# Channel mamba and merge on 65 stored columns of a row instead of 69, from compact copies written by the pixel mamba

## The chip, the cores and the metric

The kernel runs on one core of a Trainium2 chip. The metric is the device time of one execution in microseconds (us). All times are medians of several runs unless one execution is named.

## The reference, cut to what matters

A four layer network works on x of shape (4, 64, 128, 128): frequency gates with attention, a Fourier block with experts, a Hartley convolution, and a block of two mambas. The third layer ends by multiplying its result with a mask over the columns, and the fourth layer takes that as its input:

```python
freqs = jnp.fft.fftfreq(W)
mask = (jnp.abs(freqs) <= CUTOFF).astype(y.dtype)   # CUTOFF = 0.25, W = 128
return y * mask                                      # layer 2: 65 of 128 columns stay
...
def step(h, inp):
    dA_t, dBx_t, C_t = inp
    h = dA_t * h + dBx_t
    y = jnp.einsum('bds,bs->bd', h, C_t)
    return (h, y)
...
xs = x.transpose(0, 2, 3, 1).reshape(1, -1, C)              # one sequence of 65536 pixels
ys = mamba_fwd(xs, spa_in_w, ...)                            # "pixel" mamba
spa = silu(group_norm(ys, spa_gn_w, spa_gn_b, GROUPS)) + x
xe = x.transpose(0, 2, 3, 1).reshape(B * H * W, TOKEN, gcn)  # 8 tokens of 8 channels per pixel
ye = mamba_fwd(xe, spe_in_w, ...)                            # "channel" mamba
spe = x + silu(group_norm(ye, spe_gn_w, spe_gn_b, GROUPS))
w = jax.nn.softmax(att_w)
return spa * w[0] + spe * w[1] + x
```

Columns 0 to 32 and 96 to 127 are nonzero, 65 in all. In the other 63 both the input and the mamba outputs that are added are constants or zero; the pixel mamba has to carry its state over them.

## The kernel before

The program is a row of stages with a barrier of all engines behind each. A stage has one instruction stream for each engine, ordered by semaphores. DMAs are issued by SP alone. The last three stages are the ones that the change touches.

The stage before them stores x2 in DRAM with `KEPT = 69` columns for each of the 4 x 128 image rows: columns 0 to 36 and 96 to 127. The four zero columns are there for the pixel mamba: seen from column 96 of one row (`SHIFT = 32` values earlier), a "row" is 32 + 33 nonzero columns, three zero ones, and one column whose state update is replaced by a jump over the zero part of the image.

`spatial_mamba` (tiles `spa_`, the pixel mamba) walks the 512 rows in `NC = 74` chunks of `RA = 7` rows, 483 values for each of 64 channels. A chunk passes through four engines in software pipelining: the helper `stream` takes for every engine a list of (lag, part) and runs part `c - lag` in iteration c; the first `HEAD` iterations and the last ones are written out, those between are a hardware loop with four chunks in a pass. SP's parts are `next_load` (waits until `project_z` of chunk c is done, then loads chunk c + 4 in two DMAs into slot s = c % 4 of `xt`) and, three chunks behind, `store` (waits until ACT has copied the output to `res`, then writes it to `ys`). PE's parts include `project_x`, `project_out` and, right behind the latter, `project_z`, which reads `xt`; VectorE (DVE) has 16 scans (L2549), 8 products (`feed`, L2535) and one gate in a chunk.

`spectral_mamba` (tiles `spe_`, the channel mamba) treats every stored pixel by itself, in chunks of `GP = 512` pixels that pay no heed to rows: `LX = 4 * 128 * 69 = 35328` pixels are 69 chunks. `HEAD` is 9, so 14 passes of four chunks are in the hardware loop (`(69 - 9) // 4 - 1`), the rest is written out. SP loads one chunk with one DMA and stores one with another. The scans are at L2876, the products at L2865, and PE sums over states with 128x128 matmuls (L2753).

`merge_branches` (tiles `merge_`) holds `ys` and `ye` of all images in SBUF (`v0`, `v1`: eight DMAs of `K = 128 * 69` values in 64 partitions), takes statistics with 24 instructions of `BN = 368` values for each of four parts (L3011), and then in 8 turns of two strips of 16 rows loads x2 again (`xs`), applies the two SiLUs (ACT, L2974), adds (DVE, L3046 to L3056) and stores 16 full rows of 128 columns. The `L = 37` columns on the left and `LR = 32` on the right come from the sum, the 59 between them from a constant that ACT fills in (L2978).

Of the kernel before, what the change touches and what calls it, by code (L numbers as in the profile page):

```python
# [9 lines left out]
ALU = mybir.AluOpType  # L10
# [3 lines left out]
B, C, H, W = 4, 64, 128, 128  # L14
# [1933 lines left out]
M2 = 20  # L1948
KEPT = 69
PADX = 36  # L1950
# [129 lines left out]


LX = B * H * KEPT
ST = 16
TK, CG, DE = 8, 8, 16
TD = TK * DE
# [7 lines left out]

RA = 7
NA = RA * KEPT
NCA = -(-B * H // RA)
LXP = NCA * NA
JUMP = 36
SHIFT = KEPT - JUMP - 1
# [23 lines left out]


def spatial_mamba(nc, x2, w_in, w_conv, w_z, conv_b, w_xd, w_dt, dt_b, w_brep, w_crep, w_b, a_log, a_log2, skip_d, w_out, one_hot, fold, ident,
                  steady, ys):

# [3 lines left out]
    NC, UA, HEAD, NBL, NP = NCA, 4, 10, 16, 8  # L2133
    with Stage(nc, "spa") as st:
# [26 lines left out]
        xt = st.sb("xt", [128, UA, NA + 4])  # L2161
# [14 lines left out]
        res = st.sb("res", [C, 2, NA])  # L2176
# [2 lines left out]
        p_d = [st.ps(f"p_d{i}", [128, 512]) for i in range(4)]  # L2179
        p_u = st.ps("p_u", [128, 2, 512])  # L2180
        x_in, stored = [st.sem(f"x_in{s}") for s in range(UA)], st.sem2("stored")
        (loaded, step, setup_act, setup_pe, w_ready, zeroed, jump_ready, jump_out, jump_in) = (
            st.sem(n) for n in ("loaded", "step", "setup_act", "setup_pe", "w_ready", "zeroed", "jump_ready", "jump_out", "jump_in"))
        (dt_done, x_done, z_done, b_done, c_done, x_read, z_read, soft_step, soft_ready, b_copied, c_copied) = (
# [10 lines left out]
        def rows(t):  # L2195

            return t.rearrange("p (r w) -> p r w", w=KEPT)

        def jumps(t):

# [2 lines left out]
        @block.sync  # L2203
        def _(sp):
            def load(c, s):
                for q in range(2):

                    sp.dma_start(xt[q * C:(q + 1) * C, s, 0:NA + 3], x2[:, bass.ds(c * NA + (PADX - SHIFT - 3 - q), NA + 3)]).then_inc(x_in[s], 16)

            def next_load(c, s, r):  # L2210

                if isinstance(c, int) and c + UA >= NC:
                    return
                sp.wait_ge(z_done, c + 1)
                load(c + UA, s)

            def store(c, s, r):
                sp.wait_ge(out_copied, c + 1)
                sp.dma_start(ys[:, bass.ds(c * NA, NA)], res[:, s % 2, :]).then_inc(stored[s % 2], 16)

            for dst, src in ((wi[:, :, :], w_in), (wc[:, :, :], w_conv), (wz[:, :], w_z), (cb[:, 0:1], conv_b), (wxd[:, :], w_xd),
                             (wdt[:, :], w_dt), (db[:, 0:1], dt_b), (wbr[:, :], w_brep), (wcr[:, :], w_crep), (wb[:, :], w_b), (av[:, :], a_log),
                             (av2[:, :], a_log2), (dd[:, :], skip_d), (wo[:, :], w_out), (hot[:, :, :], one_hot), (fd[:, :, :], fold),
                             (idt[:, :], ident)):
                sp.dma_start(dst, src).then_inc(loaded, 16)
            for s in range(UA):
                load(s, s)

            sp.wait_ge(jump_ready, 1)
            sp.dma_start(steady.rearrange("(d s) -> d s", s=ST), jump[:, :]).then_inc(jump_out, 16)  # L2230
            sp.wait_ge(jump_out, 16)
            with nc.allow_non_contiguous_dma(reason="one column of states at the jump for each pair of strip and rows"):
                for q in range(4):
                    sp.dma_start(jump2[:, 4 * q:4 * q + 4], steady.rearrange("(g q n) -> n q g", g=4, q=4)[:, q, :]).then_inc(jump_in, 16)
            stream(sp, NC, UA, HEAD, 4, (0, next_load), (3, store))
            for s in range(2):
                sp.wait_ge(stored[s], 16 * (NC // 2))

        @block.gpsimd
        def _(pool):  # L2240
# [41 lines left out]
        def _(pe):  # L2282
# [13 lines left out]
                nc.tensor.matmul(p_x[:, 0:NA], wi[:, 1, :], xt[:, s, 1:1 + NA], start=False, stop=True).then_inc(x_done, 1)  # L2296

            def project_z(c, s, r):

                pe.wait_ge(x_read, 2 * c + 2)  # L2300
                nc.tensor.matmul(p_x[:, 0:NA], wz[:, :], xt[0:C, s, 3:3 + NA], start=True, stop=True).then_inc(z_done, 1)

# [263 lines left out]

GP, SUB = 512, 128
NSUB = GP // SUB


def spectral_mamba(nc, x2, w_in, w_conv, w_xd, w_dt, w_bc, dt_b, skip_d, a_wide, a_mask, w_out, ident, ye):
# [1 line left out]

    NC, UE, HEAD = LX // GP, 4, 9
    HALF = DE // 2 * ST * TK
    with Stage(nc, "spe") as st:
        wi = st.sb("wi", [65, 2 * TD])
# [12 lines left out]
        xt = st.sb("xt", [65, UE, GP])  # L2592
# [11 lines left out]
        res = st.sb("res", [C, 2, GP])  # L2604
# [14 lines left out]
        @block.sync  # L2619
        def _(sp):  # L2620
            def load(c, s):
                sp.dma_start(xt[0:64, s, :], x2[:, bass.ds(c * GP + PADX, GP)]).then_inc(x_in[s], 16)

            def next_load(c, s, r):

                if isinstance(c, int) and c + UE >= NC:
                    return
                sp.wait_ge(z_done, c + 1)
                load(c + UE, s)

            def store(c, s, r):
                sp.wait_ge(out_copied, c + 1)
                sp.dma_start(ye[:, bass.ds(c * GP, GP)], res[:, s % 2, :]).then_inc(stored[s % 2], 16)

            for dst, src in ((wi[:, :], w_in), (wc[:, :], w_conv), (wxd[:, :], w_xd), (wdt[:, :], w_dt), (wbc[:, :], w_bc),
                             (db[:, :], dt_b), (dd[:, :], skip_d), (wa[:, :], a_wide), (am[:, :], a_mask), (wo[:, :], w_out), (idt[:, :], ident)):
                sp.dma_start(dst, src).then_inc(loaded, 16)
            for s in range(UE):
                load(s, s)
            stream(sp, NC, UE, HEAD, 4, (0, next_load), (3, store))  # L2640
            for s in range(2):
                sp.wait_ge(stored[s], 16 * ((NC + 1 - s) // 2))
# [247 lines left out]


NR = 16
BN = 368


def merge_branches(nc, ys, ye, x2, gmat, gwb, att, out):

    K = H * KEPT  # L2900
    NS = H // NR // 2
    N = NR * KEPT
    L, LR = JUMP + 1, KEPT - JUMP - 1
    with Stage(nc, "merge") as st:
        v = [st.sb(f"v{q}", [128, 2, K]) for q in range(2)]
        xs = st.sb("xs", [128, 2, N])
# [27 lines left out]
        @block.sync  # L2934
        def _(sp):
            for dst, src in ((gm[:, :], gmat), (gw[:, :, :], gwb), (at[:, 0:2], att)):
                sp.dma_start(dst, src).then_inc(loaded, 16)
            for q, src in enumerate((ys, ye)):
                for a in range(2):
                    for p in range(2):  # L2940
                        sp.dma_start(v[q][64 * p:64 * p + 64, a, :], src[:, (2 * a + p) * K:(2 * a + p + 1) * K]).then_inc(v_in[2 * q + a], 16)  # L2941
            for a in range(2):
                @turns(sp, NS)
                def _(j):
                    for s in range(2):

                        sp.wait_ge(x_scaled[s], a * NS + j)
                        for p in range(2):
                            sp.dma_start(xs[64 * p:64 * p + 64, s, :], x2[:, bass.ds((2 * j + s) * N + (PADX + (2 * a + p) * K), N)])\  # L2949
                                .then_inc(x_in[s], 16)  # L2950
                    for s in range(2):
                        sp.wait_ge(merged[s], a * NS + j + 1)
                        sp.wait_ge(filled[s], a * NS + j + 1)
                        sp.dma_start(ov[:, a, bass.ds((2 * j + s) * NR, NR), :], os[:, s]).then_inc(stored[s], 16)  # L2954
            for s in range(2):
                sp.wait_ge(stored[s], 32 * NS)
# [31 lines left out]
        def _(dve):  # L2988
# [29 lines left out]
            r = K / HW  # L3018
# [20 lines left out]
            for a in range(2):  # L3039
                @turns(dve, NS)  # L3040
                def _(j):
                    for s in range(2):
# [7 lines left out]
                        dve.wait_ge(added[s], a * NS + j + 1)  # L3050

                        dve.wait_ge(stored[s], 16 * (a * NS) + 16 * j)
                        tv = tx[:, :].rearrange("p (r w) -> p r w", w=KEPT)
                        sv = t2[:, s, :].rearrange("p (r w) -> p r w", w=KEPT)
                        nc.vector.scalar_tensor_tensor(os[:, s, :, 0:L], sv[:, :, 0:L], at[:, 4:5], tv[:, :, 0:L], ALU.mult, ALU.add)  # L3055
                        nc.vector.scalar_tensor_tensor(os[:, s, :, W - LR:W], sv[:, :, L:KEPT], at[:, 4:5], tv[:, :, L:KEPT], ALU.mult,  # L3056
                                                       ALU.add).then_inc(merged[s], 1)


# [150 lines left out]
def shape_constants():  # L3210
# [65 lines left out]
    "kd": (B, 99, 1280, BF16), "vd": (B, 128, VC), "den": (4, NH, 512), "qp": (3, B, C, HW, BF16), "x1": (B, C, H, W), "st1": (B, C, 32, 6),  # L3276
    "low1": (2 * MD, B * C, MD), "modes1": (2, B, C, MD, MD), "ab1": (C, 2, B), "y1": (B * C, H, W), "feats": (128, 2, HW),
    "fmean": (128, 2), "sel": (B, TOP, NE), "wts": (B, TOP), "out1": (B, C, H, W), "low2": (2 * MD, B * C, MD),
    "modes2": (2, B, C, M2 + 1, M2 + 1), "x2": (C, NCA * NA + 8), "ys": (C, LXP), "steady": (128 * ST,), "ye": (C, LX),
}  # L3280


# [9 lines left out]
def build(nc, t, out):  # L3292
# [7 lines left out]
    def of(names):  # L3300
        return [t[n] for n in names.split()]
# [19 lines left out]
    hartley_modes(nc, *of("low2 t_re t_im half wm mixc modes2 x2"))  # L3321
    low_inverse(nc, "inv2", t["modes2"], M2 + 1, *of("c_k2 c_m2"), t["x2"][:, PADX:PADX + LX].rearrange("c (b h w) -> h b c w", b=B, h=H))

    spatial_mamba(nc, *of("x2 a_in a_conv a_z a_cb a_xd a_dt a_dtb a_brep a_crep a_b a_alog a_alog2 a_d a_out one_hot fold_states ident steady ys"))
    spectral_mamba(nc, *of("x2 e_in e_conv e_xd e_dt e_bc e_dtb e_d e_alog decay_mask e_out ident ye"))
    merge_branches(nc, t["ys"][:, SHIFT:SHIFT + LX], *of("ye x2 groups16 m_gn m_att"), out)


# [13 lines left out]
```

## Time and profile before

| what | value |
|---|---|
| median of 3 runs | 7990.96 us (7986.05 to 7993.15) |
| the profiled execution | 7999.3 us |
| its span, first to last instruction | 7997.2 us |
| TensorE | 6916.9 us busy, 86% of the span |
| VectorE | 5842.8 us busy, 73% |
| ScalarE | 4018.5 us busy, 50% |
| GpSimd | 3606.3 us busy, 45% |
| pixel mamba, from the first load to the next stage | 3696 to 5753 us, 2057 us |
| channel mamba | 5753 to 7766 us, 2013 us |
| merge | 7766 to 7997.2 us, 231.2 us |

The busy shares are means over all stages. The three stages at the end fill just over half of the span, and each has another limit, so they are read one at a time.

### The profile page before, as it was taken

How to read it: one execution, taken by the hardware profiler on the slowest of the kernel's cores; microseconds unless marked ns; L12 is line 12 of the kernel's file. 1: busy time of each engine (PE TensorE's matmuls, PEld its weight loads, DVE VectorE, ACT ScalarE, POOL GpSimd, SP SyncE). 2: the span in 40 equal slices, each digit the busy share in tenths (PEclk: the TensorE clock that was granted, in tenths of full speed). 3: DMA queues.
4: the chain of work that ended last, by engine and by line, in shares of the span. 5: the costliest groups of instructions: out<-in, count | busy, mean ns of one | idle time of the engine just before them, and what ended most of it. 6: DMA issues, size and time to landing. Idle time of an engine off the chain costs nothing. (4 is left out here: it accounts for less than half of the span.)

```text
span 7997.2 us, 123173 instructions
## 1 busy us (share of the span) xinstructions
PE 6916.9 (86%) x38274; PEld 3725.9 (47%) x38274; DVE 5842.8 (73%) x5708; ACT 4018.5 (50%) x6797; POOL 3606.3 (45%) x2432
## 2 busy tenths in 40 slices
PE   8959479999987369787999999999899999999970
PEld 7845223333335224574222222222277777777760
DVE  4630468777742258213999999999899999999975
ACT  4410456666641357202666666666555555555532
POOL 0100012222210300002777777777688888888860
PEclk9979789999988689756999999999899999999985
DMA  2252443333335623532000000000000000000016
GB/s 71 68 124 46 164 131 100 99 102 100 100 108 123 244 99 103 133 84 46 14 15 13 14 14 13 15 13 14 13 10 11 10 10 10 10 10 11 10 37 188
DMA packets 555088, 500.09 MB, mean 63 GB/s; under 512 B 222861, under 2 KB 462388, under 8 KB 547788
## 3 DMA queue, kind: packets, MB, share of 16 engines
q1 hardware_dynamic: 554763, 495.54, 23.0%
q8 instruction: 232, 3.80, 0.2%
q14 instruction: 93, 0.75, 0.0%
HBM read 328.99 MB, written 163.76 MB: 62 GB/s over the span
## 5 line engine op out<-in xcount | busy, mean ns | idle before, releaser
L2549 DVE TENSOR_TENSOR_SCAN spa_hs<-spa_p_d,spa_hs,spa_bx 128x483 f32<-128x483 f32 x1168 | 1634.5, 1676 | 0.0
L2679 POOL TENSOR_TENSOR spe_hc<-spe_hs,spe_cu 128x1024 f32<-128x1024 f32 x552 | 1291.9, 2361 | 312.5 <-DVE spe_hs L2876 312.5
L2275 POOL TENSOR_TENSOR spa_hc<-spa_hs,spa_cr 128x966 f32<-128x966 f32 x592 | 1223.9, 2068 | 427.7 <-DVE spa_hs L2549 411.6
L2876 DVE TENSOR_TENSOR_SCAN spe_hs<-spe_p_d,spe_bx 128x1024 f32<-128x1024 f32 x552 | 1232.8, 2275 | 46.6 <-ACT spe_p_d L2825 45.9
L2753 PE MATMUL spe_p_y<-spe_idt,spe_hc 128*128 128x128 f32 x8832 | 1036.1, 276 | 0.0
L2753 PEld LDWEIGHTS spe_p_y<-spe_idt,spe_hc 128*128 128x128 f32 x8832 | 1013.9, 193 | 0.0
L1070 DVE TENSOR_REDUCE attention_nm<-attention_p_s 128x2 f32<-128x640 f32 x1024 | 789.2, 812 | 259.2 <-PE attention_p_s L927 258.1
L2535 DVE TENSOR_TENSOR spa_bx<-spa_br,spa_p_u 128x952 f32<-128x952 f32 x592 | 938.2, 1585 | 33.7 <-PE spa_p_u L2345 33.7
L1028 ACT ACTIVATE attention_pr<-attention_p_t 128x512 f32<-128x512 f32 x1280 | 710.6, 598 | 411.7 <-PE attention_p_t L950 285.8
L2825 ACT ACTIVATE spe_p_d<-spe_p_d 128x896 f32<-128x896 f32 x552 | 474.1, 900 | 869.8 <-PE spe_p_d L2738 869.4
L2460 ACT ACTIVATE spa_p_d<-spa_p_d,spa_av 128x483 f32<-128x483 f32 x1184 | 705.1, 634 | 409.8 <-PE spa_p_d L2332 407.7
L2332 PE MATMUL spa_p_d<-spa_du,spa_hot 32*128 32x483 f32 x2368 | 644.4, 619 | 58.0 <-DVE spa_hs L2549 48.8
L2865 DVE TENSOR_TENSOR spe_bx<-spe_cu,spe_p_bc 128x2048 f32<-128x2048 f32 x276 | 631.5, 2288 | 53.4 <-ACT spe_cu L2817 17.0
L2345 PE MATMUL spa_p_u<-spa_du,spa_hot 32*128 32x483 f32 x2368 | 646.9, 621 | 0.6 <-DVE spa_bx L2535 0.5
L927 PE MATMUL attention_p_s<-attention_ks,attention_qs 96*128 96x320 bf16 x2048 | 454.5, 303 | 37.2 <-DMA attention_qs<-scratch_qp 21.1
L1133 POOL TENSOR_TENSOR attention_on<-attention_os,attention_rc 128x512 f32<-128x512 f32 x128 | 162.3, 1268 | 602.4 <-DMA attention_rc<-scratch_den 381.6
L2332 PEld LDWEIGHTS spa_p_d<-spa_du,spa_hot 32*128 32x128 f32 x2368 | 182.0, 184 | 523.1 <-DVE spa_hs L2549 360.6
L967 PE MATMUL attention_p_o<-attention_pr,attention_vs 128*32 128x512 f32 x3072 | 410.0, 606 | 0.4 <-ACT attention_os L1042 0.4
L2738 PE MATMUL spe_p_d<-spe_wa,spe_dt 32*128 32x512 f32 x2208 | 386.8, 640 | 16.9 <-issue 14.0
L950 PE MATMUL attention_p_t<-attention_qs,attention_ks 99*128 99x512 bf16 x1024 | 395.7, 387 | 4.8 <-DMA attention_qs<-attention_mr 3.3
L1902 PE MATMUL experts_p_x<-experts_fs,experts_wx 128*128 128x512 f32 x768 | 331.8, 595 | 47.6 <-DVE experts_bx L1928 47.6
L2359 PE MATMUL spa_p_y<-spa_hc,spa_fd 128*32 128x483 f32 x2368 | 303.6, 585 | 5.4 <-POOL spa_hc L2275 4.2
(423 smaller groups left out, 10807.0 us busy)
## 6 DMA issues: line engine op xcount, KB each, us to landing
attention_qs<-scratch_qp SPq DMA_DIRECT2D x768, 64.0 KB, 2.6
attention_rc<-scratch_den SPq DMA_DIRECT2D x128, 256.0 KB
scratch_qp<-queries_parts SPq DMA_DIRECT2D x96, 256.0 KB, 2.5
spa_xt<-scratch_x SPq DMA_DIRECT2D x148, 121.5 KB, 2.6
front_xs<-in_x_dram SPq DMA_DIRECT2D x64, 256.0 KB, 2.9
scratch_xf<-front_out SPq DMA_DIRECT2D x64, 256.0 KB, 2.3
queries_xs<-scratch_xf SPq DMA_DIRECT2D x32, 512.0 KB, 4.5
attention_xs<-in_x_dram SPq DMA_DIRECT2D x128, 128.0 KB, 4.2
```

The source lines that it names most:

```text
L1028: nc.scalar.activation(pr[:, v, :], p_t[v % 2][:, :], ACT.Exp, scale=HD ** -0.5).then_inc(exp_done[v % 2], 1)
L1070: nc.vector.tensor_reduce(nm[:, c.u, t, 2 * s:2 * s + 2], p_s[s][:, :, 0:NK], AX.X, ALU.max, negate=True).then_inc(s_max[s], 1)
L2275: nc.gpsimd.tensor_tensor(hc[:, k % 8:k % 8 + 2, :], hs[:, k:k + 2, :], cr2[:, s % 2, :].unsqueeze(1).broadcast_to([128, 2, NA]), ALU.mult ...
L2332: mm = nc.tensor.matmul(p_d[(2 * j + e) % 4][:, 0:NA], hot[v, j // 2, :], du[v, s % 2, 0, :], start=True, stop=True)
L2345: mm = nc.tensor.matmul(p_u[:, e, 0:NA], hot[v, j // 2, :], du[v, s % 2, 1, :], start=True, stop=True)
L2460: nc.scalar.activation(p_d[k % 4][:, 0:NA], p_d[k % 4][:, 0:NA], ACT.Exp, scale=av2[:, k:k + 1]).then_inc(decay_ready, 1)
L2535: nc.vector.tensor_tensor(kept(bx[:, 2 * j:2 * j + 2, :]), b, kept(p_u[:, :, 0:NA]), ALU.mult).then_inc(bx_ready, 1)
L2549: nc.vector.tensor_tensor_scan(hs[:, k, v], p_d[k % 4][:, v], bx[:, k, v], 0.0 if start else hs[:, k, NA - 1:NA], ALU.mult, ALU.add).then_ ...
L2679: nc.gpsimd.tensor_tensor(hc[:, k, :, d, :].rearrange("p s d t -> p d s t"), hs[:, k % 2, d, :, :], rows, ALU.mult)\
L2753: mm = nc.tensor.matmul(p_y[:, px], hc[:, k, n].rearrange("p d t -> p (d t)"), idt[:, :], start=False, stop=(n == ST - 1))
L2865: nc.vector.tensor_tensor(bx[:, k % 2], steps, rows, ALU.mult).then_inc(bx_ready, 1)
L2876: nc.vector.tensor_tensor_scan(hs[:, k % 2, d].rearrange("p d s t -> p (d s t)"), p_d[h][:, :], bx[:, k % 2, d].rearrange("p d s t -> p (d ...
```

## The change

The pixel mamba writes its output `ys` without the four zero columns of each row (`full`, 65 of 69 values; 7 pieces of 65 values for each channel, packed in DRAM), and writes a packed copy of its input, `xf2`, from the slot `xt` in which the chunk stands (`keep_x`). `project_z` waits until that copy has landed, since its completion is what lets `next_load` overwrite the slot. The channel mamba reads `xf2` instead of x2 and has `LF = 4 * 128 * 65 = 33280` pixels, 65 chunks. The merge reads packed `ys`, `ye` and `xf2`; its strips are 16 x 65 values, the statistics run in 20 instructions of 416 values instead of 24 of 368, and the parts of the output row are 33, 63 and 32 columns wide instead of 37, 59 and 32.

```diff
+FULL = KEPT - 4
+NF = RA * FULL
...
         x_in, stored = [st.sem(f"x_in{s}") for s in range(UA)], st.sem2("stored")
+        x_kept = [st.sem(f"x_kept{s}") for s in range(UA)]
...
+        def full(t):
+            return rows(t)[:, :, 0:FULL]
...
             def store(c, s, r):
                 sp.wait_ge(out_copied, c + 1)
-                sp.dma_start(ys[:, bass.ds(c * NA, NA)], res[:, s % 2, :]).then_inc(stored[s % 2], 16)
+                sp.dma_start(ys[:, bass.ds(c * NF, NF)], full(res[:, s % 2, :])).then_inc(stored[s % 2], 16)
+
+            def keep_x(c, s, r):
+                sp.wait_ge(x_in[s], 32 * r + 32)
+                sp.dma_start(xf2[:, bass.ds(c * NF, NF)], full(xt[0:C, s, 3:3 + NA])).then_inc(x_kept[s], 16)
...
-            stream(sp, NC, UA, HEAD, 4, (0, next_load), (3, store))
+            stream(sp, NC, UA, HEAD, 4, (0, keep_x), (0, next_load), (3, store))
             for s in range(2):
                 sp.wait_ge(stored[s], 16 * (NC // 2))
+            for s in range(UA):
+                sp.wait_ge(x_kept[s], 16 * ((NC + UA - 1 - s) // UA))
...
             def project_z(c, s, r):
-
+                pe.wait_ge(x_kept[s], 16 * r + 16)
                 pe.wait_ge(x_read, 2 * c + 2)
...
+LF = B * H * FULL
...
-    NC, UE, HEAD = LX // GP, 4, 9
+    NC, UE, HEAD = LF // GP, 4, 9
...
-                sp.dma_start(xt[0:64, s, :], x2[:, bass.ds(c * GP + PADX, GP)]).then_inc(x_in[s], 16)
+                sp.dma_start(xt[0:64, s, :], x2[:, bass.ds(c * GP, GP)]).then_inc(x_in[s], 16)
...
-BN = 368
+BN = 416
...
-    K = H * KEPT
+    K = H * FULL
     NS = H // NR // 2
-    N = NR * KEPT
-    L, LR = JUMP + 1, KEPT - JUMP - 1
+    N = NR * FULL
+    L, LR = FULL - SHIFT, SHIFT
...
+    nonzero = t["xf2"][:, SHIFT:SHIFT + LF]
+    spectral_mamba(nc, nonzero, *of("e_in e_conv e_xd e_dt e_bc e_dtb e_d e_alog decay_mask e_out ident ye"))
+    merge_branches(nc, t["ys"][:, SHIFT:SHIFT + LF], t["ye"], nonzero, *of("groups16 m_gn m_att"), out)
```

On SP, at the top of the pixel mamba's loop, one chunk, in the kernel before. An ISA row is a wait or a register step, REGISTER_ALU computes an address.

```order
L2116 ISA
L2208 ISA
L2208 DMA spa_xt<-scratch_x 64x486
L2208 REGISTER_ALU
L2208 DMA spa_xt<-scratch_x 64x486
L2218 REGISTER_ALU
L2219 ISA
L2219 DMA scratch_ys<-spa_res 64x483
```

The same place in the changed kernel, up to the copy of the next chunk; `scratch_xf` stands for `xf2` here:

```order
L2118 ISA
L2229 ISA
L2229 DMA scratch_xf<-spa_xt 64x7x65
L2220 REGISTER_ALU
L2214 ISA
L2214 DMA spa_xt<-scratch_x 64x486
L2214 REGISTER_ALU
L2214 DMA spa_xt<-scratch_x 64x486
L2224 REGISTER_ALU
L2225 ISA
L2225 DMA scratch_ys<-spa_res 64x7x65
L2229 ISA
```

The copy stands ahead of the chunk's `next_load`, so behind the store of the iteration before; nothing else on SP moved.

On PE, in the same loop, around `project_z` (it reads `spa_wz`), before:

```order
L2345 MATMUL spa_p_u<-spa_du,spa_hot 128x483 x2
L2365 MATMUL spa_p_y<-spa_y,spa_wo 64x483
L2300 ISA
L2301 MATMUL spa_p_x<-spa_xt,spa_wz 128x483
L2091 REGISTER_ALU
L2332 MATMUL spa_p_d<-spa_du,spa_hot 128x483 x2
```

and in the changed kernel:

```order
L2357 MATMUL spa_p_u<-spa_du,spa_hot 128x483 x2
L2377 MATMUL spa_p_y<-spa_y,spa_wo 64x483
L2311 ISA
L2312 ISA
L2313 MATMUL spa_p_x<-spa_xt,spa_wz 128x483
L2092 REGISTER_ALU
L2344 MATMUL spa_p_d<-spa_du,spa_hot 128x483 x2
```

One row is new, the wait for the copy. The rows of VectorE, ScalarE and GpSimd are as many as before (2046, 2011 and 869): the channel mamba's code is the same, with one pass less of its loop.

## Rows read from the trace of the kernel before

**Rows 1.** The page's first line

```profile
span 7997.2 us, 123173 instructions
```

**Rows 2.** Windows: stretch and its length, busy us of each engine, clock, DMA share, GB/s

```profile
3760.00:5700.00 1940.00, 1882.64 (x8085) 565.60 (x8081) 1939.72 (x1808) 1265.47 (x2094) 1523.41 (x870) 1.00 0.05 13
5850.00:7650.00 1800.00, 1770.66 (x12134) 1343.32 (x12132) 1727.69 (x821) 967.41 (x1579) 1493.46 (x759) 0.99 0.04 10
7768.00:7855.00 87.00, 0.00 (x0) 0.00 (x0) 37.14 (x79) 1.58 (x2) 0.00 (x0) 0.50 1.00 210
```

**Rows 3.** Groups of instructions, channel mamba: busy, mean ns, idle before, releaser

```profile
L2876 DVE TENSOR_TENSOR_SCAN spe_hs<-spe_p_d,spe_bx 128x1024 f32<-128x1024 f32 x552 | 1232.8, 2275 | 46.6 <-ACT spe_p_d L2825 45.9
```

**Rows 4.** Timeline of SP, channel mamba: start, length, DMA issued

```profile
6111.31 0.49 SPq L2622 DMA_DIRECT2D spe_xt<-scratch_x  x1
...
6139.11 0.50 SPq L2622 DMA_DIRECT2D spe_xt<-scratch_x  x1
...
6226.47 0.49 SPq L2622 DMA_DIRECT2D spe_xt<-scratch_x  x1
...
7486.15 0.49 SPq L2622 DMA_DIRECT2D spe_xt<-scratch_x  x1
```

**Rows 5.** Timeline of SP and PE, pixel mamba, one chunk

```profile
4275.73 0.52 SPq L2219 DMA_DIRECT2D scratch_ys<-spa_res  x1
...
4300.01 1.07 PE L2301 MATMUL spa_p_x<-spa_xt,spa_wz 64*128 64x483 f32 x2
...
4302.66 0.52 SPq L2219 DMA_DIRECT2D scratch_ys<-spa_res  x1
```

**Rows 6.** The tile spa_res: its DMA issues and time to landing, min/median/max

```profile
L2219 SPq DMA_DIRECT2D scratch_ys<-spa_res x74: 466/519/603, 3792.2 to 5747.3; - x74
DMA to landing us min/median/max: 2.2/2.3/3.0
```

**Rows 7.** DMA, 3560 to 3680 us, the stage before: packets, MB, share of 16 engines

```profile
q1 hardware_dynamic: 38572, 8.67, 53.5%
```

**Rows 8.** Timeline of SP and PE, start of the pixel mamba

```profile
3717.18 2.02 SPq L2234 DMA_DIRECT2D spa_jump<-scratch_steady  x4
...
3726.40 1.07 PE L2301 MATMUL spa_p_x<-spa_xt,spa_wz 64*128 64x483 f32 x2 [1.39 <-ACT spa_sg L2414]
...
3727.50 1.11 SPq L2208 DMA_DIRECT2D spa_xt<-scratch_x  x2
...
3741.36 1.17 PE L2301 MATMUL spa_p_x<-spa_xt,spa_wz 64*128 64x483 f32 x1 [1.31 <-ACT spa_sg L2414]
```

**Rows 9.** Waits in the pixel mamba, 3760 to 5700 us: us in total, times, longest

```profile
PEld spa_p_d L2332 <- DVE spa_hs L2549: 360.6, 420, 1.1
```

**Rows 10.** The tile spa_xt: SP's register steps at its loads, ns min/median/max

```profile
L2208 SPq MOVE spa_xt<-scratch_x x120: 29/29/29, 3979.0 to 5563.8; - x120
```

**Rows 11.** Timeline, end of the pixel mamba to the next stage's first DMA

```profile
5747.31 0.47 SPq L2219 DMA_DIRECT2D scratch_ys<-spa_res  x1
5753.45 0.35 SPq L2637 DMA_DIRECT2D spe_wi<-in_e_in_dram  x1
```

**Rows 12.** Timeline of DVE, merge, the last statistics

```profile
7855.94 12.26 DVE L3011 BATCH_NORM_STATS2 merge_bs<-merge_v 128x6 f32<-128x368 f32 x24 [9.54 <-DMA merge_v<-scratch_ye]
7868.23 2.79 DVE L3015 BATCH_NORM_AGGREGATE merge_mv<-merge_bs 128x2 f32<-128x144 f32 x4
```

**Rows 13.** Timeline of DVE, merge, one of the 8 turns and the start of the next

```profile
7892.66 0.80 DVE L3046 TENSOR_SCALAR merge_tx<-merge_xs,merge_at 128x1104 f32<-128x1104 f32 x1 [7.22 <-DMA merge_xs<-scratch_x]
7893.49 1.37 DVE L3049 SCALAR_TENSOR_TENSOR merge_tx<-merge_t,merge_at,merge_tx 128x1104 f32<-128x1104 f32 x1
7894.99 0.84 DVE L3055 SCALAR_TENSOR_TENSOR merge_os<-merge_t,merge_at,merge_tx 128x592 f32<-128x592 f32 x1
7895.74 0.74 DVE L3056 SCALAR_TENSOR_TENSOR merge_os<-merge_t,merge_at,merge_tx 128x512 f32<-128x512 f32 x1
...
7907.41 0.80 DVE L3046 TENSOR_SCALAR merge_tx<-merge_xs,merge_at 128x1104 f32<-128x1104 f32 x1 [7.01 <-DMA merge_xs<-scratch_x]
```

More of the change, by code:

```diff
@@ L2125, in spatial_mamba @@
 def spatial_mamba(nc, x2, w_in, w_conv, w_z, conv_b, w_xd, w_dt, dt_b, w_brep, w_crep, w_b, a_log, a_log2, skip_d, w_out, one_hot, fold, ident,
-                  steady, ys):
+                  steady, ys, xf2):
     NC, UA, HEAD, NBL, NP = NCA, 4, 10, 16, 8
@@ L2948, in _ @@
                         for p in range(2):
-                            sp.dma_start(xs[64 * p:64 * p + 64, s, :], x2[:, bass.ds((2 * j + s) * N + (PADX + (2 * a + p) * K), N)])\
+                            sp.dma_start(xs[64 * p:64 * p + 64, s, :], x2[:, bass.ds((2 * j + s) * N + (2 * a + p) * K, N)])\
                                 .then_inc(x_in[s], 16)
@@ L3052, in _ @@
                         dve.wait_ge(stored[s], 16 * (a * NS) + 16 * j)
-                        tv = tx[:, :].rearrange("p (r w) -> p r w", w=KEPT)
-                        sv = t2[:, s, :].rearrange("p (r w) -> p r w", w=KEPT)
+                        tv = tx[:, :].rearrange("p (r w) -> p r w", w=FULL)
+                        sv = t2[:, s, :].rearrange("p (r w) -> p r w", w=FULL)
                         nc.vector.scalar_tensor_tensor(os[:, s, :, 0:L], sv[:, :, 0:L], at[:, 4:5], tv[:, :, 0:L], ALU.mult, ALU.add)
-                        nc.vector.scalar_tensor_tensor(os[:, s, :, W - LR:W], sv[:, :, L:KEPT], at[:, 4:5], tv[:, :, L:KEPT], ALU.mult,
+                        nc.vector.scalar_tensor_tensor(os[:, s, :, W - LR:W], sv[:, :, L:FULL], at[:, 4:5], tv[:, :, L:FULL], ALU.mult,
                                                        ALU.add).then_inc(merged[s], 1)
@@ L3278 @@
     "fmean": (128, 2), "sel": (B, TOP, NE), "wts": (B, TOP), "out1": (B, C, H, W), "low2": (2 * MD, B * C, MD),
-    "modes2": (2, B, C, M2 + 1, M2 + 1), "x2": (C, NCA * NA + 8), "ys": (C, LXP), "steady": (128 * ST,), "ye": (C, LX),
+    "modes2": (2, B, C, M2 + 1, M2 + 1), "x2": (C, NCA * NA + 8), "ys": (C, NCA * NF), "xf2": (C, NCA * NF), "steady": (128 * ST,), "ye": (C, LF),
 }
@@ L3322, in build @@
     low_inverse(nc, "inv2", t["modes2"], M2 + 1, *of("c_k2 c_m2"), t["x2"][:, PADX:PADX + LX].rearrange("c (b h w) -> h b c w", b=B, h=H))
-    spatial_mamba(nc, *of("x2 a_in a_conv a_z a_cb a_xd a_dt a_dtb a_brep a_crep a_b a_alog a_alog2 a_d a_out one_hot fold_states ident steady ys"))
-    spectral_mamba(nc, *of("x2 e_in e_conv e_xd e_dt e_bc e_dtb e_d e_alog decay_mask e_out ident ye"))
-    merge_branches(nc, t["ys"][:, SHIFT:SHIFT + LX], *of("ye x2 groups16 m_gn m_att"), out)
+    spatial_mamba(nc, *of("x2 a_in a_conv a_z a_cb a_xd a_dt a_dtb a_brep a_crep a_b a_alog a_alog2 a_d a_out one_hot fold_states ident steady ys xf2"))
+    nonzero = t["xf2"][:, SHIFT:SHIFT + LF]
+    spectral_mamba(nc, nonzero, *of("e_in e_conv e_xd e_dt e_bc e_dtb e_d e_alog decay_mask e_out ident ye"))
+    merge_branches(nc, t["ys"][:, SHIFT:SHIFT + LF], t["ye"], nonzero, *of("groups16 m_gn m_att"), out)
 def kernel(**inputs):
```

## The prediction

> **What bounds the kernel now.** The last three stages are read apart, from windows inside each. In the pixel mamba VectorE is busy for 1939.72 of 1940 us, first row of [rows 2]: it never waits, so whatever else is added there is free as long as VectorE still never waits. In the channel mamba TensorE is busy for 1770.66 of 1800 us and VectorE for 1727.69, second row: the two are nearly balanced, VectorE's scans lose only 46.6 us to waits in the whole stage [rows 3], and no queue of transfers matters at 10 GB/s. A stage like that is as long as its number of chunks times one period. The merge first waits for memory: DMA share 1.00 at 210 GB/s, third row of [rows 2]. Then VectorE takes statistics of the last part to arrive [rows 12], and after a few short operations come 8 turns that alternate between the load of x and VectorE [rows 13].
>
> **The channel mamba, the main term.** It has 65 chunks instead of 69. Head and tail are written out and stay, so exactly one pass of four chunks leaves the loop. The timeline of its loads gives the price [rows 4]: the first load of a pass is issued at 6111.31 and that of the next at 6226.47; twelve passes lie between 6111.31 and 7486.15, so (7486.15 - 6111.31) / 12 = 114.6 us a pass. Inside a pass one chunk takes 6139.11 - 6111.31 = 27.8 us; four would be 111.2, and the other 3.4 us are the jump back at the end of a pass, which leaves with it. I take -114.6. The bounds are 111.2 (the jump's cost stays somewhere) and 115.2 (6226.47 - 6111.31, a long pass). Nothing in the instructions of a chunk changes, since a chunk is 512 pixels in either kernel.
>
> **The merge.** Its eight big loads carry 8 x 64 x 8832 x 4 B = 18.09 MB before and 8 x 64 x 8320 x 4 B = 17.04 MB after. At 210 GB/s, [rows 2], the 1.05 MB are 5.0 us. The last statistics are 24 instructions in 12.26 us [rows 12], 511 ns each for 368 values. 20 of 416 values take 12.26 x 20/24 = 10.2 us if an instruction costs the same whatever its width, and 12.26 x 8320/8832 = 11.5 if only the values count; I take 11.1 between them, -1.1 (bounds -2.0 and -0.7). The aggregation reads 120 numbers instead of 144: at most 2.79 / 6, I take -0.4. A turn of the loop takes 7907.41 - 7892.66 = 14.75 us [rows 13], of which 7 are VectorE's wait for x. For each strip, L3046 and L3049 run over 1040 instead of 1104 values and L3055 over 528 instead of 592. The slope comes from L3055 and L3056: 0.84 us for 592 and 0.74 for 512 is about 1.2 ns a value. So L3049 and L3055 lose 64 x 1.2 ns = 0.08 us each, L3046 by its proportion 0.80 x 64/1104 = 0.05: 0.21 us a strip, 0.42 a turn. x itself: the two loads of a strip carry 0.565 MB, and 64/1104 of that, 33 KB, goes; only the first strip's loads are waited for, and 33 KB at 210 GB/s are 0.15 us. 0.55 us a turn with rounding down, -4.4 in 8 turns; the bounds are -2.5 (only the bytes count: 66 KB a turn, 0.3 us x 8) and -6.8 (everything shrinks by 64/1104: 14.75 x 0.058 x 8). ACT's fill of 63 columns instead of 59 is not on this chain: ACT has the 7 us for it in which VectorE waits.
>
> **The pixel mamba, what is added.** 74 copies `keep_x`, 74 stores that now have 448 pieces of 260 B instead of 64 of 1932 B, and a wait on TensorE. First the copy. It is issued right behind the store of the iteration before, which is at 4275.73 + 0.52 = 4276.3; `project_z`, which waits for it, starts at 4300.01 [rows 5]. The cover is 23.7 us. SP's wait for `x_in` in front of it costs nothing, for that load was issued three chunks earlier. What does the copy take? A store to DRAM lands in 2.3 us [rows 6]. Small pieces are priced by the stage before, where 38572 packets of 225 B on average took 53.5% of 16 engines for 120 us [rows 7]: 0.535 x 120 x 16 / 38572 = 26.6 ns a packet, so 448 of them on 16 engines are 0.75 us. 2.3 + 0.75 = 3 us against 23.7: hidden, with more than 20 us to spare. Without that cover every us would cost 74. Behind the copy on SP stand the two loads of `next_load`, some 0.6 us later than now, for data needed four chunks later, and the store, whose buffer is wanted two chunks later. In the fill of the pipeline the iterations are shorter: the copy of chunk 0 follows the jump transfers at 3717.18 + 2.02 and has 7 us until 3726.40, and that of chunk 1 follows the loads at 3727.50 + 1.11 and has 12 us until 3741.36 [rows 8]. Both hold 3 us easily.
>
> The wait itself is one more row on TensorE in the loop. The nearest price is a register step of 29 ns [rows 10]. TensorE's weight loads waited 360.6 us for VectorE's scans in the window [rows 9], some 5 us a chunk, so I take 0; two such steps on the path in each chunk would be 4.3 us, my upper bound.
>
> A rule of the Trainium skill speaks against the short pieces. [Rows 7] show 26.6 ns for a packet of 225 B, that is 8.5 GB/s for an engine where the long rows of the merge have 210/16 = 13 GB/s. DMA: Bandwidth & Descriptors, Specifications, says that 512 B or more are needed for line rate and that below this the engine reads, modifies and writes. The trace agrees that short pieces are slower, by a third here. By the row the sum is as it stands; if the rule doubled the price of a packet, the last store would land 0.75 us later still and nothing else would change.
>
> At the end of the stage the last store lands 0.75 us later, and SP waits for it. Between its issue and the next stage there are 6.1 us now [rows 11], of which 2.3 are the landing; the other 3.8 hold the clearing of 41 semaphores by GpSimd and the barrier, so four more semaphores are 0.3 us. Together +1.0 (bounds 0.3 and 1.8).
>
> **The sum.** -114.6 - 5.0 - 1.1 - 0.4 - 4.4 + 1.0 = -124.5 us against the profiled execution of 7999.3 us (span 7997.2 [rows 1]): 7874.8. The median of the runs is 8.3 us below the profiled one, so 7990.96 - 124.5 = 7866.5 us.
>
> **Rivals.**
> The copy is late (slower). If the copy landed after `project_z` is due, TensorE would stand still there with the spreads of the same chunk queued behind it, VectorE would starve, and each us late would cost 74. It decides at a landing 23.7 + 124.5 / 74 = 25.4 us after the issue; at 27 us (3.3 us late) the time is 7866.5 + 244 = 8111. Against it: the packets would have to cost 30 times what [rows 7] show. 3%.
> VectorE is disturbed. Its scans fill the pixel mamba completely, and there are now 148 transfers of short pieces that read SBUF beside them. If that, or the extra row on TensorE, made a chunk 0.2 us longer, it would be 15 us: 7881. For it: nothing in the stage has slack on VectorE. Against it: the stage's DMA share is 0.05 [rows 2], and 2 x 0.75 us in each 26.9 us (4302.66 - 4275.73, [rows 5]) adds as much again. 7%.
> The merge loads run slower. Their rows in DRAM have other lengths (33280 B, and a pitch of 134680 B for `ys` and `xf2` instead of near 143000). At 160 GB/s instead of 210 the 17.04 MB take 106.5 us instead of 86.1 before: 20.4 + 5.0 us are lost from the sum, 7892. For it there is nothing in the rows but that the layout changes. 4%.
> The change doesn't do what it says. Then the loop would run as many passes as before; the chunk count is computed from `LF`, and the order of instructions shows unchanged code for the compute engines, so this needs an error that I don't see. Under 1%, counted with the first.
>
> **How the numbers follow.** The forecast has 86%. Its own bounds: the gains are at most 115.2 + 5.2 + 2.0 + 0.5 + 6.8 - 0.3 = 129.4 (7861.6) and at least 111.2 + 4.6 + 0.7 + 0 + 2.5 - 1.8 - 4.3 = 112.9 (7878.1), where 4.6 and 5.2 are the 1.05 MB at 10% more or less bandwidth on either side. The runs of before scatter by 7 us, half of it to either side; that and the disturbed VectorE widen it to 7857 to 7884. 0.2%, 16 us, is about what a measurement of this kernel can tell from no change. Forecast, disturbed VectorE and slow merge loads all lie far beyond it on the fast side, 97%, of which I keep 1% for a mix that ends near no change. Faster 96%, the same 1%, slower 3%.
>
> **What would show it.** The channel mamba's stage, 2013 us now, should be near 1898 with 27.8 us between loads inside a pass and thirteen passes. The pixel mamba should have VectorE busy for all of a window in its middle, 26.9 us a chunk, and no wait of TensorE for a DMA to `scratch_xf`; the copy's landing should be near 3 us. The merge should be near 220 us with a turn of 14.2. It would be wrong if the pixel mamba's chunks grew, if a pass of the channel mamba had another length under the same code, or if the big loads fell below 210 GB/s.

## The result, and the profile after

The changed kernel takes 7900.06 us (median of 4 runs, 7894.98 to 7901.65), the kernel before 7988.51 (4 runs); the ratio is 0.9888 with a 95% interval of 0.987 to 0.9905. It is faster by 88.5 us, where 124.5 were forecast, and the time lies above the range of 7857 to 7884. The profiled execution of after has a span of 7893.2 us.

From the first DMA of one stage to the first of the next (`spa_wi`, `spe_wi`, `merge_gm`), and the forecast for each:

| stage | before | after | change | forecast |
|---|---|---|---|---|
| all before the pixel mamba | 3695.2 | 3677.8 | -17.4 | 0 |
| pixel mamba | 2058.2 | 2061.6 | +3.4 | +1.0 |
| channel mamba | 2012.0 | 1932.9 | -79.1 | -114.6 |
| merge | 231.8 | 220.9 | -10.9 | -10.9 |

The first line is code that both kernels share, and the two profiled executions stand on different sides of their medians (7999.3 against 7988.51, 7894.98 against 7900.06). The other three add up to -86.6, and that is the 88.5 of the medians within 2 us. So the merge came out as worked out, the pixel mamba nearly so, and the channel mamba gave 35.5 us less than one pass of its loop.

The channel mamba's loads in the timeline of SP, as in [rows 4]:

```profile
6100.77 0.48 SPq L2635 DMA_DIRECT2D spe_xt<-scratch_xf  x1
...
6128.60 0.49 SPq L2635 DMA_DIRECT2D spe_xt<-scratch_xf  x1
...
6217.68 0.49 SPq L2635 DMA_DIRECT2D spe_xt<-scratch_xf  x1
```

A chunk inside a pass still takes 6128.60 - 6100.77 = 27.8 us, but a pass takes 6217.68 - 6100.77 = 116.9, and over ten passes from 6067.52 to 7243.34 the mean is 117.6 (before, between the same loads, 114.55). Four chunks in a row are 111.5, so the jump back costs 6.1 us a pass instead of 3.0 (the prediction has 3.4, since it counts four times 27.8 us, where four chunks take 111.5). Twelve intervals that are 3.1 us longer are 37 us: the part that is missing.

The timeline of TensorE shows where. First the kernel before, at the top of a pass:

```profile
6208.47 1.13 PE L2738 MATMUL spe_p_d<-spe_wa,spe_dt 32*128 32x512 f32 x4 [1.19 <-issue]
6209.53 0.90 PE L2726 MATMUL spe_p_bc<-spe_wbc,spe_xz 128*128 128x256 f32 x2
```

and the changed one:

```profile
6197.94 1.13 PE L2751 MATMUL spe_p_d<-spe_wa,spe_dt 32*128 32x512 f32 x4 [1.17 <-issue]
6200.90 1.19 PE L2739 MATMUL spe_p_bc<-spe_wbc,spe_xz 128*128 128x256 f32 x2 [1.84 <-issue]
```

"issue" is idle time in which the engine waited for no semaphore that the profile shows. Before there is one such gap behind the jump, after there are two. VectorE, which is busy for nearly all of a pass, then stands still until ScalarE has the next decay. The waits of VectorE's scans, in us, times and the longest, first before (6000 to 7600 us), then after (6000 to 7500 us):

```profile
DVE spe_hs L2876 <- ACT spe_p_d L2825: 38.1, 14, 3.5
DVE spe_hs L2889 <- ACT spe_p_d L2838: 62.0, 14, 5.8
```

In both executions there are transfers of the kind "instruction" in every pass. The DMA view of the changed kernel, 6067 to 6525 us (four passes of 117.6 less a little), has the same row as that of the kernel before, 6080 to 6538 us:

```profile
q8 instruction: 36, 0.59, 0.5%
```

36 packets of 0.59 MB / 36 = 16.4 KB, nine in a pass. The view doesn't name the engine that they belong to; the experiments show that it is TensorE's place that decides on them.

The pixel mamba, one chunk on SP and PE as in [rows 5]:

```profile
4287.28 1.26 SPq L2214 DMA_DIRECT2D spa_xt<-scratch_x  x2
4288.80 0.68 SPq L2225 DMA_DIRECT2D scratch_ys<-spa_res  x1
4289.67 0.67 SPq L2229 DMA_DIRECT2D scratch_xf<-spa_xt  x1
...
4312.86 1.07 PE L2313 MATMUL spa_p_x<-spa_xt,spa_wz 64*128 64x483 f32 x2
```

The copy is issued by 4290.3 and needed at 4312.86, 22.5 us later; the packed stores of `spa_res` land in a median of 3.5 us (2.3 before, [rows 6]):

```profile
DMA to landing us min/median/max: 3.1/3.5/4.0
```

Windows of the changed kernel: a quarter of the pixel mamba, and the big loads of the merge, as in [rows 2]:

```profile
4240.00:4740.00 500.00, 485.17 (x2084) 145.10 (x2084) 500.00 (x467) 325.44 (x539) 393.10 (x224) 1.00 0.08 17
...
7675.00:7757.00 82.00, 0.00 (x0) 0.00 (x0) 31.38 (x67) 1.58 (x2) 0.00 (x0) 0.50 1.00 207
```

VectorE is busy without a gap, the DMA share rises from 0.05 to 0.08, and the merge loads keep their rate. The merge's other terms, as in [rows 12, 13]:

```profile
7758.05 10.24 DVE L3024 BATCH_NORM_STATS2 merge_bs<-merge_v 128x6 f32<-128x416 f32 x20 [10.36 <-DMA merge_v<-scratch_ye]
7768.32 2.36 DVE L3028 BATCH_NORM_AGGREGATE merge_mv<-merge_bs 128x2 f32<-128x120 f32 x4
...
7791.72 0.76 DVE L3059 TENSOR_SCALAR merge_tx<-merge_xs,merge_at 128x1040 f32<-128x1040 f32 x1 [7.02 <-DMA merge_xs<-scratch_xf]
...
7806.11 0.76 DVE L3059 TENSOR_SCALAR merge_tx<-merge_xs,merge_at 128x1040 f32<-128x1040 f32 x1 [7.00 <-DMA merge_xs<-scratch_xf]
```

A turn takes 7806.11 - 7791.72 = 14.4 us, the statistics 10.24 us, the aggregation 2.36.

One reading trap: the page of the changed kernel gives the pixel mamba's scan a mean of 1197 ns where before it is 1676, though VectorE fills its windows in both and a chunk takes 26.85 us in both. Such means of overlapping VectorE records are no basis for a sum; the distance between two chunks is.

### The profile page after: what moved, and what is told of

The parts are those of the page before. It is cut to its first block and busy times, and to the rows that moved or that the text cites. A ratio compares the mean times of both kernels' runs of the same rounds, so it can differ in the third digit from the quotient of the medians.

```text
span 7893.2 us, 121220 instructions
## 1 busy us (share of the span) xinstructions
PE 6796.0 (86%) x37506; PEld 3630.6 (46%) x37506; DVE 5722.7 (73%) x5640; ACT 3956.5 (50%) x6697; POOL 3509.9 (44%) x2384
## 5 line engine op out<-in xcount | busy, mean ns | idle before, releaser
L2561 DVE TENSOR_TENSOR_SCAN spa_hs<-spa_p_d,spa_hs,spa_bx 128x483 f32<-128x483 f32 x1168 | 1355.3, 1197 | 0.0
L2692 POOL TENSOR_TENSOR spe_hc<-spe_hs,spe_cu 128x1024 f32<-128x1024 f32 x520 | 1215.0, 2357 | 295.2 <-DVE spe_hs L2889 295.2
L2889 DVE TENSOR_TENSOR_SCAN spe_hs<-spe_p_d,spe_bx 128x1024 f32<-128x1024 f32 x520 | 1161.9, 2275 | 68.5 <-ACT spe_p_d L2838 67.7
L2766 PE MATMUL spe_p_y<-spe_idt,spe_hc 128*128 128x128 f32 x8320 | 977.9, 276 | 0.0
L2766 PEld LDWEIGHTS spe_p_y<-spe_idt,spe_hc 128*128 128x128 f32 x8320 | 957.0, 193 | 0.0
L2838 ACT ACTIVATE spe_p_d<-spe_p_d 128x896 f32<-128x896 f32 x520 | 446.6, 900 | 820.2 <-PE spe_p_d L2751 819.9
L2547 DVE TENSOR_TENSOR spa_bx<-spa_br,spa_p_u 128x952 f32<-128x952 f32 x592 | 659.3, 1114 | 35.1 <-PE spa_p_u L2357 35.0
L2878 DVE TENSOR_TENSOR spe_bx<-spe_cu,spe_p_bc 128x2048 f32<-128x2048 f32 x260 | 594.9, 2288 | 60.7 <-ACT spe_cu L2830 27.8
L2751 PE MATMUL spe_p_d<-spe_wa,spe_dt 32*128 32x512 f32 x2080 | 364.8, 641 | 17.9 <-issue 14.6
```

The costliest lines, as they stand in the source:

```text
L2547: nc.vector.tensor_tensor(kept(bx[:, 2 * j:2 * j + 2, :]), b, kept(p_u[:, :, 0:NA]), ALU.mult).then_inc(bx_ready, 1)
L2561: nc.vector.tensor_tensor_scan(hs[:, k, v], p_d[k % 4][:, v], bx[:, k, v], 0.0 if start else hs[:, k, NA - 1:NA], ALU.mult, ALU.add).then_ ...
L2692: nc.gpsimd.tensor_tensor(hc[:, k, :, d, :].rearrange("p s d t -> p d s t"), hs[:, k % 2, d, :, :], rows, ALU.mult)\
L2766: mm = nc.tensor.matmul(p_y[:, px], hc[:, k, n].rearrange("p d t -> p (d t)"), idt[:, :], start=False, stop=(n == ST - 1))
L2878: nc.vector.tensor_tensor(bx[:, k % 2], steps, rows, ALU.mult).then_inc(bx_ready, 1)
L2889: nc.vector.tensor_tensor_scan(hs[:, k % 2, d].rearrange("p d s t -> p (d s t)"), p_d[h][:, :], bx[:, k % 2, d].rearrange("p d s t -> p (d ...
```

## The experiments

**The theories.** P (place): the wait in `project_z` adds instructions to TensorE's stream ahead of the channel mamba, so its loop lies elsewhere in the stream, and the price of the jump depends on that. L (loads): something in the data, the packed source of the loads or the smaller number of chunks, lengthens a pass. In the trace of the changed kernel the new wait (L2312) is an instruction of its own for 14 chunks that are written out, and a pass of the pixel mamba's loop has two register steps more on TensorE: the loop of the channel mamba lies 16 instructions later than before.

**The wait on SP** (`sp_wait`), the changed kernel with

```diff
             def next_load(c, s, r):
...
                 sp.wait_ge(z_done, c + 1)
+                sp.wait_ge(x_kept[s], 16 * r + 16)
                 load(c + UA, s)
...
             def project_z(c, s, r):
-                pe.wait_ge(x_kept[s], 16 * r + 16)
                 pe.wait_ge(x_read, 2 * c + 2)
```

> The changed kernel with one thing moved: the wait for the copy of x stands on SP, ahead of the load that overwrites the slot, and not on TensorE ahead of project_z. TensorE's instruction stream in front of the channel mamba's loop is then as long as in the kernel before. Theory P (the place of TensorE's loop in its instruction stream sets the cost of the jump back): a pass of the channel mamba takes 114.6 us again instead of 117.6, its stage about 1894 instead of 1933, and the time is about 38 us below that of the changed kernel, near 7862. Rival L (the loads from the packed copy, or anything else in the data): the pass stays at 117.6 and the time near 7900.

Measured: 7863.42 us, ratio to before 0.9848 (0.9832 to 0.9865). The pass is 114.8, the channel stage 7642.0 - 5743.7 = 1898.3. All data and copies are those of the changed kernel; only where the wait stands differs. That speaks for P. The time is 121.1 us below the kernel before on the same chip (7984.5), where the changed kernel had 88.5 and the forecast 124.5: 32.6 of the 36.0 us that were missing are back.

**The kernel before, its loop moved** (`before_shift16`):

```diff
             pe.wait_ge(w_ready, 4)
             pe.wait_ge(zeroed, 1)
+            for _ in range(32):
+                pe.wait_ge(w_ready, 4)
```

> The kernel before, with 32 more waits (long satisfied) on TensorE at the start of the channel mamba, two of which make one instruction, so that its loop lies 16 instructions later in the stream, as in the changed kernel. Data, copies and chunk count are those of before. Theory P: a pass takes 117.6 us instead of 114.6, 14 passes add some 40 us, near 8028. Rival L: nothing but well under 1 us for the waits themselves, 7989.

Measured: 8033.32 us against 7984.5 on the same chip, ratio 1.0063 (1.0046 to 1.008), and a pass of 117.8. Sixteen instructions that do nothing cost the kernel 49 us. In the profiled executions the channel stage has 41 of them (2053.4 against 2012.0); the rest lies elsewhere and isn't explained. L is out as the explanation: neither copy nor chunk count has changed here.

**Only the chunk count** (`before_65`), which leaves out the last 2048 stored pixels in the channel mamba:

```diff
-    NC, UE, HEAD = LX // GP, 4, 9
+    NC, UE, HEAD = 65, 4, 9
...
-                        sp.dma_start(v[q][64 * p:64 * p + 64, a, :], src[:, (2 * a + p) * K:(2 * a + p + 1) * K]).then_inc(v_in[2 * q + a], 16)
+                        k0 = (2 * a + p) * K - (4 * GP if q and a and p else 0)
+                        sp.dma_start(v[q][64 * p:64 * p + 64, a, :], src[:, k0:k0 + K]).then_inc(v_in[2 * q + a], 16)
```

> The kernel before, in which the channel mamba handles 65 chunks of the 69-column copy instead of 69 and leaves out the last 2048 stored pixels (the merge reads earlier ones in their place). Code lengths are those of before. Theory P and the prediction's main term: the channel stage falls by one pass of 114.6 us, from 2012 to about 1898, pass length 114.6. If the passes themselves get longer with fewer chunks, the stage is near 1933.

Measured: 7880.7 us in one run (7999.3 in the profiled execution of before), the stage 7646.2 - 5752.1 = 1894.1 us, 117.9 below before, with a pass of 114.45. The main term of the prediction holds when the place is kept.

**The changed kernel, moved on** (`after_shift16`: the same 32 waits in the changed kernel).

> The changed kernel with 32 more long-satisfied waits on TensorE at the start of the channel mamba, so that the loop lies 32 instructions later than in the kernel before and 16 later than in the changed one. Theory P: the pass length changes again, to a value that depends on where the loop's start and end fall; if the cost is periodic in 16 instructions it stays at 117.6, otherwise anything between 112 and 121. Rival L: 117.6.

Measured: 7820.02 us in one run, and the cost of the jump is gone: 111.5 a pass. The DMA view of it over 458 us in the loop has

```profile
q1 hardware_dynamic: 2720, 4.46, 4.0%
q8 instruction: 1, 0.02, 0.0%
```

One instruction packet instead of 36. So P is right in its main point, and the guess that it might repeat every 16 is wrong.

**Further places**, all with such waits at the start of the channel mamba: 32 instructions in the kernel before (`before_shift32`), 8 and 24 in the changed one, which make 24 and 40 in all.

> The kernel before with 64 more long-satisfied waits on TensorE at the start of the channel mamba: its loop lies 32 instructions later. Theory P: only the place counts, so the jump costs nothing here either, as in the changed kernel 32 instructions behind the place of before: a pass of 111.4 us, and 14 of them give back 44 us: near 7940. If the vanished jump needed the other data or the other chunk count, the pass stays at 114.6 or 117.7.

> The changed kernel with 8 more instructions of waits on TensorE at the start of the channel mamba, 24 in all beyond before. Theory P in its simple form (a block of the stream is fetched at the jump and another when its end is crossed): the pass is either 117.7 as at 16 or 111.4 as at 32, or a value between, if part of the fetch is hidden; time 7820 to 7900.

> The changed kernel with 24 more instructions of waits on TensorE at the start of the channel mamba, 40 in all beyond before. Theory P says that 32 is not a single point: a pass of 111.4 here too, time near 7820, or, if the free range is narrow, a pass of 114 or more and 7850 or more.

Measured: 7942.31 us with a pass of 111.5; 7903.61 with 119.5; 7802.94 with 111.5. The cost of the jump is 3.0 us at the place of before, 6.1 at 16 instructions and 8.0 at 24, and is gone at 32 and 40. At 32 it is gone with either source of the loads and either count of chunks. These are single runs, whose times also hold what the stages ahead happened to take: the times of `after_shift8` and the changed kernel hardly differ, though a pass is 1.9 us longer. The pass and the stage are compared, not the time.

**A rule for it.** The queue moves packets of 256 instructions, if an instruction is 64 B (which no run measures, but the return after 256 below fits), and a pass of the loop has 1647 (the trace has 768 weight loads and 768 matmuls, two of each for one matmul of the program, and 111 others). Theory B: if the loop touches at most 7 blocks of 256, nothing is fetched again, otherwise all of it in every pass. Four runs test it, the kernel before with 144, 176, 208 and 256 instructions.

> The kernel before with TensorE's channel loop 144 instructions later. The traces so far show, besides the pass lengths, that the instruction queue moves 36 packets of 16.4 KB in four passes where the jump costs time and none where it is free; 16.4 KB are 256 instructions of 64 B, and the loop has 384 matmuls of four instructions each and 111 others, 1647 in all, 6.4 such packets. Theory B (the loop stays loaded if it touches no more than 7 blocks of 256, and is fetched anew in every pass if it touches 8): it starts on a new block between 24 and 32, so it is free for 256 x 7 - 1647 = 145 instructions behind that point, and 144 is still free: a pass of 111.5, no instruction packets in the passes, near 7945. Rival U (each place has a cost of its own without such a rule): any value.

> The same with 176 instructions. Theory B: at the very edge of the free range (169 to 177 by its count), so a pass of 111.5, or just beyond it if the count is off by a few; this run finds the edge, 7945 or above 7970.

> The same with 208 instructions. Theory B: beyond the free range, the loop touches 8 blocks again: instruction packets in every pass and a pass of 112 to 120 us. Rival U: any value; a theory in which the jump is free everywhere behind 32 says 111.5.

> The same with 256 instructions, one whole packet. Theory B: all repeats, the pass is 114.5 us as in the kernel before, plus at most 2 us in all for the waits at the start of the stage. Without a period of 256, nothing ties it to 114.5.

Measured: 7944.38, 7965.15, 7992.61 and 7998.45 us, one run each, and 7963.7 in one run of the kernel before on that chip. All places together, with the pass as the mean over ten, the instruction packets in some four passes, and the whole channel stage (69 chunks in the kernels named before, 65 in the others):

| loop later by | kernel | pass, us | packets | stage, us |
|---|---|---|---|---|
| 0 | before | 114.55 | 36 | 2012.0 |
| 0 | sp_wait | 114.8 | 36 | 1898.3 |
| 16 | after | 117.6 | 36 | 1932.9 |
| 16 | before_shift16 | 117.8 | 36 | 2053.4 |
| 24 | after_shift8 | 119.5 | 35 | 1959.2 |
| 32 | after_shift16 | 111.5 | 1 | 1861.6 |
| 32 | before_shift32 | 111.5 | 1 | 1974.7 |
| 40 | after_shift24 | 111.5 | none | 1863.9 |
| 144 | before_shift144 | 111.5 | none | 1985.4 |
| 176 | before_shift176 | 113.3 | 9 | 2008.4 |
| 208 | before_shift208 | 114.1 | 36 | 2028.9 |
| 256 | before_shift256 | 114.9 | 36 | 2041.0 |

The rows of the instruction queue for 176 and 208 (for 144 the view has no such row):

```profile
q8 instruction: 9, 0.15, 0.2%
```

```profile
q8 instruction: 36, 0.59, 0.5%
```

Free from 32 to at least 144, back at 208, and at 256 nearly the pass of 0: each as the rule says. At 176, the edge, 113.3 is a mean of two kinds of pass. The loads of `before_shift176` that open a pass:

```profile
6097.13 0.49 SPq L2622 DMA_DIRECT2D spe_xt<-scratch_x  x1
...
6215.11 0.49 SPq L2622 DMA_DIRECT2D spe_xt<-scratch_x  x1
...
6326.61 0.49 SPq L2622 DMA_DIRECT2D spe_xt<-scratch_x  x1
```

The first pass takes 118.0 us, the next 111.5. Of 13 such intervals three are long (116.7 to 118.0) and the others 111.5 or 111.7. Each long one goes with nine instruction packets, four of them before the interval ends and five in the next one, and 6327 to 6661 us has none. So even at the edge a jump has its code fetched in full or not at all; why it falls one way or the other there isn't known.

One expectation was far off: "at most 2 us in all for the waits at the start of the stage". From the stage's first DMA to the same load of chunk 13 it is 243.3 us in the kernel before, 246.8 with 32 idle instructions, 257.7 with 144 and 270.8 with 256. An idle instruction costs some 0.1 us there, 27.5 us for 256, which is why the stage of `before_shift256` is 29 us longer than that of before with nearly the same pass.

**The best version** (`best`): `sp_wait` with 64 such waits, 32 instructions.

> The changed kernel with the wait for the copy on SP instead of TensorE, and 64 long-satisfied waits (32 instructions) on TensorE at the start of the channel mamba, which put its loop 32 instructions behind its place in before. Theory P: no cost of the jump, a pass of 111.4, 7820 us, some 165 below the kernel before. Under the rival that the wait's own position matters, it would be off from that by as much as sp_wait was from the changed kernel.

Measured: 7818.87 us (4 runs) against 7971.86 on that chip, ratio 0.9808 (0.9789 to 0.9827), a pass of 111.5. The change alone has 0.9888, so this is 0.8% below it, and below both kernels. Its stage takes 1863.7 us.

## Why the prediction was wrong, point by point

**The step that failed** is in the main term: "the other 3.4 us are the jump back at the end of a pass, which leaves with it", with the bounds of 111.2 and 115.2. It took the price of the jump for a constant of the loop, and counted only the one that leaves. The runs show that it depends on where TensorE's loop lies in the stream, and the change moved it by 16 instructions: the 12 jumps that stay cost 3.1 us more each, 37 us, and the stage gave 79.1 us, far below the lower bound. The sentence "Nothing in the instructions of a chunk changes" was true and did not protect the term. Together with "The wait itself is one more row on TensorE", costed at 0 to 4.3 us, it shows the hole: the wait was priced where it executes, and there it costs nothing that can be seen; it was not asked what its length does to everything behind it in the stream. `sp_wait`, with the same data and no such instructions, gains 121.1 us of the 124.5 forecast. So this one step is nearly the whole miss; the pixel mamba's +3.4 us instead of +1.0 may be most of what is left. The prediction named the sign of it, that "a pass of the channel mamba had another length under the same code", but gave that no price and no chance.

**Leaving out four chunks** was right: `before_65` saves 117.9 us of stage against 114.6. Of the other 3.3 us, 1.0 are in the twelve passes that both have and 2.3 behind the loop, in one execution of each.

**The merge** is -10.9 as forecast, and that it fits so well is luck, as the parts show: statistics 12.26 to 10.24 us, -2.0 where -1.1 was taken and -2.0 was the bound for "an instruction costs the same whatever its width" (512 ns each, before 511, so that bound is the fact); aggregation -0.4 as taken; the turn 14.75 to 14.4, -2.9 in eight where -4.4 was taken. Up to the last statistics it is 85.7 us instead of 90.5, -4.8 where -5.0 was taken for the loads, which ran at 207 GB/s. The four parts make -10.1; the other 0.8 us lie between them. One bound of the loads was miscalculated: 5.0 us at 10% less bandwidth are 5.6, not 5.2, which moves the 7861.6 by 0.4 us and changes nothing here.

**The copy** was right. It had 22.5 us of cover. The view doesn't list its landing apart, but a store of the same shape lands in 3.5 us, and no DMA to `scratch_xf` stands among what TensorE waited for. The landing of a packed store rose by 1.2 us where 0.75 was worked out from the price of a packet, and the end of the stage by the same: from the last store to the next stage 7.3 us instead of 6.1. The Trainium skill (DMA: Bandwidth & Descriptors, Specifications) says that transfers below 512 B are done as read-modify-write. It has no price for that; with a packet's price doubled, which is the prediction's own assumption, the estimate would be 1.5, and the measured value lies between. But the 26.6 ns of [rows 7] come from packets of 225 B and so hold this cost already, if there is one: where the other 0.45 us come from stays open. The pixel stage grew by 3.4 us in all; variants of both kernels have 2057.9 to 2061.1, so the rest of it can't be told from scatter.

**The rivals.** The late copy and the slow merge loads did not happen. A disturbed VectorE in the pixel mamba did not either: 26.85 us a chunk and no gap in the middle of the stage. None of the rivals was the real one, a longer jump. It was within reach: [rows 4] show that 3.4 us of a pass belong to no chunk, and the page of the kernel before has a queue of the kind "instruction":

```profile
q8 instruction: 232, 3.80, 0.2%
```

## What to carry to other kernels

Where a loop's body is long, read the kind "instruction" in the DMA view inside the loop. If there are packets in every pass, code is fetched again each time, and then an edit anywhere ahead on that engine, a wait in another stage too, can change the time of the loop: here 16 idle instructions by +49 us, and 32 by 37 us of the channel stage the other way (7707.7 - 5733.0 = 1974.7 against 2012.0). Compare two versions only after the place of such loops has been looked at, and place waits on an engine whose stream has no such loop behind it; a few idle instructions are a cheap way to move one: 32 cost 3.5 us ahead of the loop here and gave back 40 in it.

## What the runs showed that was not expected

TensorE's loop of 1647 instructions runs without any fetch when it starts between 32 and at least 144 instructions behind its place in the kernel before, and has nine packets of 16.4 KB a pass at 0, 16, 24, 208 and 256, for 2.6 to 8.0 us a pass. The return at 256 and both edges fit the rule that a loop stays loaded when it touches at most seven blocks of 256 instructions. That is inferred from these nine places of one loop; how large the store is, and whether another loop keeps to the rule, isn't shown. Why the price climbs from 3.0 to 8.0 us between 0 and 24 was not tried. The second gap of TensorE (1.84 us) ahead of L2739 suggests that a second piece of code is waited for: in the changed kernel single instruction packets start at 6194 to 6196, 6198 to 6199 and 6201.5 to 6204 us, and the two gaps end at 6197.94 and 6200.90, and the later the loop starts in its block, the sooner the next one is needed. This is argued, not tested. The nine packets are one or two more than the seven or eight blocks, and whether these are code fetched ahead stays open.
